# The first chunk of a mixture-of-experts kernel by eight plain products instead of seven Strassen-Winograd ones

## The reference, cut to what matters

```python
def _L0_cond_ref(h, gating_probs, shared_gate_prob, Wg, Wu, Wd, Sg, Su, Sd):
    g = jnp.einsum('bsd,edf->ebsf', h, Wg)          # 8 experts, D=256, F=1024
    u = jnp.einsum('bsd,edf->ebsf', h, Wu)
    expert_outs = jnp.einsum('ebsf,efd->ebsd', jax.nn.silu(g) * u, Wd)
    expert_output = jnp.einsum('be,ebsd->bsd', gating_probs, expert_outs)
    shared = jnp.einsum('bsf,fd->bsd', jax.nn.silu(h @ Sg) * (h @ Su), Sd)
    sg = shared_gate_prob[:, :, None]
    return (1.0 - sg) * expert_output + sg * shared
x = x + _L0_cond_ref(x, fside_Bx8_0, condB_sharedgateprob[:, None], ...)   # x is (16, 256, 256) f32
```

## Time and profile before

| | us |
|---|---|
| median of three runs | 2104.42 |
| the profiled execution | 2105.31 |
| its span, first to last instruction | 2103.5 |
| PE busy in it | 2091.9 (99%) |
| POOL busy | 1611.3 (77%) |
| DVE busy | 1447.7 (69%) |
| ACT busy | 1304.2 (62%) |
| DMA, mean | 206 GB/s |

### The profile page before, as it was taken

One profiled execution on the slowest core, in us unless ns is written; L12 is line 12 of the kernel. 1 busy time (PEld: TensorE's weight loads), 2 busy tenths in 40 slices (PEclk: granted clock), 3 DMA queues, 4 the chain that ended last, 5 costly groups with the idle time before them and its releaser, 6 DMA issues.

```text
span 2103.5 us, 33963 instructions
## 1 busy us (share of the span) xinstructions
PE 2091.9 (99%) x9183; PEld 1719.2 (82%) x9183; DVE 1447.7 (69%) x2630; ACT 1304.2 (62%) x2335; POOL 1611.3 (77%) x1442
## 2 busy tenths in 40 slices
PE   8999999999999999999999999999999999999999
PEld 6888888888888888888888888888888888888887
DVE  7666666666666666666676666666667666666666
ACT  7777777777566555555556655555555555555555
POOL 7988887877488777777778877777777778777776
PEclk9999999999999999999999999999999999999999
DMA  6976666666555455445445446445445445545443
GB/s 221 349 245 238 234 242 230 242 229 232 203 197 209 173 215 209 173 194 209 174 193 210 177 191 229 178 188 209 180 186 210 184 184 210 203 183 209 183 183 143
DMA packets 122747, 433.94 MB, mean 206 GB/s; under 512 B 13760, under 2 KB 41792, under 8 KB 122688
## 3 DMA queue, kind: packets, MB, share of 16 engines
q1 hardware_dynamic: 122688, 433.32, 54.9%
HBM read 329.85 MB, written 103.28 MB: 206 GB/s over the span
## 4 chain that ended last, share of the span: by engine, by line
PE 99%; DVE 1%; issue 0%; ACT 0%; DMA 0%; DVEq 0%; ACTq 0%
PE chain_ps L684 15%; PE chain_ps L685 15%; PE chain_ps L686 15%; PE down_ps L686 8%; PE down_ps L685 8%; PE down_ps L684 8%; PE p_ps L684 6%; PE p_ps L686 6%; PE p_ps L685 6%; PE side_ps L686 4%; PE side_ps L685 4%; PE side_ps L684 4%; DMA acc<-xT 0%; ACT h_forms L1089 0%; DVE acc L1232 0%
## 5 line engine op out<-in xcount | busy, mean ns | idle before, releaser
L455 POOL TENSOR_TENSOR h_forms<-h_t,h_forms 128x512 fp32r<-128x512 f32 x429 | 560.5, 1325 | 269.1 <-ACT h_forms L1089 269.1
L684 PE MATMUL chain_ps<-x_hi,gate_forms 128*128 128x512 f32 x1080 | 422.5, 391 | 0.2
L686 PE MATMUL chain_ps<-x_hi,gate_forms 128*128 128x512 f32 x1080 | 420.7, 390 | 0.0
L685 PE MATMUL chain_ps<-x_lo,gate_forms 128*128 128x512 f32 x1080 | 420.7, 390 | 0.0
L455 POOL TENSOR_TENSOR h_t<-h_b,h_t 128x512 f32<-128x512 f32 x214 | 312.1, 1458 | 73.5 <-DVE h_b L1226 58.2
L1232 DVE TENSOR_TENSOR p_ps<-tap_p,chain_ps 128x512 f32<-128x512 f32 x216 | 150.4, 696 | 247.5 <-PE chain_ps L686 247.5
L1103 ACT COPY chain_ps<-chain_ps 128x512 f32<-128x512 f32 x216 | 123.1, 570 | 281.6 <-DVE h_a L1226 193.9
L1089 ACT CAST h_forms<-h_t 128x512 fp32r<-128x512 f32 x429 | 267.3, 623 | 15.1 <-POOL h_t L455 3.6
L455 POOL TENSOR_TENSOR w_lo<-w_raw,w_hi 128x1152 fp32r<-128x1152 f32 (+2 forms) x74 | 191.9, 2594 | 78.1 <-ACT w_hi L984 77.6
L684 PEld LDWEIGHTS chain_ps<-x_hi,gate_forms 128*128 128x128 f32 x1080 | 202.5, 188 | 54.8 <-ACT chain_ps L1103 5.3
L686 PEld LDWEIGHTS chain_ps<-x_hi,gate_forms 128*128 128x128 f32 x1080 | 202.7, 188 | 43.2
(11 more groups left out here) (117 smaller groups left out, 4878.0 us busy)
## 6 DMA issues: line engine op xcount, KB each, us to landing
gate_forms<-kept_gate SPq DMA_DIRECT2D x216, 896.0 KB, 7.4
down_forms<-kept_down SPq DMA_DIRECT2D x108, 896.0 KB, 4.6
kept_gate<-w_hi SPq DMA_DIRECT2D x72, 448.0 KB, 2.5
kept_gate<-w_lo SPq DMA_DIRECT2D x72, 448.0 KB, 3.1
w_raw<-w SPq DMA_DIRECT2D x72, 256.0 KB, 3.0
w_raw<-w SPq DMA_DIRECT2D x72, 128.0 KB, 2.8
kept_down<-d_hi SPq DMA_DIRECT2D x36, 256.0 KB, 2.3
kept_down<-d_lo SPq DMA_DIRECT2D x36, 256.0 KB, 2.8
```

Of the source, the lines that this page charges most:

```text
L455: return nc.gpsimd.tensor_tensor(dst, a, b, ALU.subtract)
L684: nc.tensor.matmul(bank, w_high, hi, start=start, stop=False, **on)
L685: nc.tensor.matmul(bank, w_high, lo, start=False, stop=False, **on)
L686: return nc.tensor.matmul(bank, w_low, hi, start=False, stop=stop, **on)
```

## The change

Chunk 0 of group 0 is no longer computed by the seven products. PE does eight plain products, `plain_chunk`: 24 matmuls in place of 21. Its first product is written out, and each of its three matmuls waits for its own operand only. The results are gate and up themselves, so that ACT applies the silu straight from the accumulators and the taps, gate sums and up sum of unit 0 go. Chunk 0's S sums are still needed for the stored weights: POOL makes them first thing (`plain_chunk_sums`), and DVE casts and subtracts them late (end of `first_steps`). The lo part of chunk 1's A11, A12 moves from POOL to DVE. B12, until now not needed, gets a hi and a lo part. p4 of unit 0 is gone from between p5 and p6 of unit 1. Chunk 0's stores by SP come behind other loads. All counts of semaphores that unit 0 no longer raises are one lower (`PLAIN`); such lines are left out but for one. Blank lines are left out too.

```diff
-FIRST_X_HI = (B11, T1, B21, B22, T2, T3, T4)
+FIRST_X = (B11, B21, B22, T1, T2, T3, T4)
+PLAIN = 1
...
             def first_keeps():
+                sp.wait_ge(w_lo_done, 1)
+                sp.wait_ge(w1_gate_lo_done, 1)
+                load_blocks(0, 5)
+                sp.wait_ge(w_lo_done, 2)
+                load_blocks(0, 6)
                 sp.wait_ge(w0_lo_done, 4)
                 load_blocks(0, 4)
-                sp.wait_ge(w_lo_done, 1)
-                load_blocks(0, 5)
                 keep_gate(0, 0)
-                keep_down(0, 0)
-                sp.wait_ge(w_lo_done, 2)
-                load_blocks(0, 6)
-                sp.wait_ge(w1_lo_done, 2)
+                sp.wait_ge(w1_lo_done, 1)
                 sp.wait_ge(d_sums, 4)
                 load_down(0, 4)
                 load_down(0, 5)
+                keep_down(0, 0)
...
+            def plain_chunk_sums():
+                def step(dst, a, b, op):
+                    nc.gpsimd.tensor_tensor(raw_of(0, dst, dst), raw_of(0, a, a), raw_of(0, b, b), op).then_inc(w0_sums, 1)
+                pool.wait_ge(w0_lo_done, 2)
+                step(S1, A21, A22, ALU.add)
+                step(S3, A11, A21, ALU.subtract)
+                pool.wait_ge(w0_sums, 1)
+                step(S2, S1, A11, ALU.subtract)
+                pool.wait_ge(w0_sums, 3)
+                step(S4, A12, S2, ALU.subtract)
             def first_chunks():
+                plain_chunk_sums()
                 next_sums(0, 0)
-                pool.wait_ge(w1_hi_done, 1)
-                part_lo(1, A11, A12).then_inc(w1_lo_done, 1)
+                coefficients()
                 pool.wait_ge(w_hi_done, 1)
                 part_lo(1, S3, S4).then_inc(w_lo_done, 1)
-                coefficients()
                 next_sums(0, 1)
                 next_sums(0, 2)
+                pool.wait_ge(w_hi_done, 2)
+                part_lo(2, D0, A22)
                 pool.wait_ge(w_hi_done, 3)
-                part_lo(2, D0, A22)
+                part_lo(2, S1, S4).then_inc(w_lo_done, 1)
                 pool.wait_ge(w_hi_done, 4)
-                part_lo(2, S1, S4).then_inc(w_lo_done, 1)
                 part_lo(1, D0, D1).then_inc(w1_lo_done, 1)
...
             def p4(g, k, n, first=False):
-                pe.wait_ge(up1_done, n + 1)
+                pe.wait_ge(up1_done, n + 1 - PLAIN)
...
             def p1_of(n, k):
                 s = k % SLOTS
-                opening = isinstance(n, int) and n == 0
-                if opening:
-                    first_w(0)
-                elif isinstance(n, int) and n == 1:
-                    pe.wait_ge(w1_lo_done, 1)
+                if isinstance(n, int) and n == 1:
+                    pe.wait_ge(w1_gate_lo_done, 1)
+                    pe.wait_ge(silu_done[0], 1)
                 else:
                     pe.wait_ge(w_lo_done, n)
-                after(pe, h_lo_done[0], n - 1)
-                product(chain_ps[:, k % 2, :], made(s, A11), x_of(0, B11, opening), start=True, stop=True).then_inc(p1_done, 1)
+                    pe.wait_ge(h_lo_done[0], n - 1)
+                product(chain_ps[:, k % 2, :], made(s, A11), x_of(0, B11, False), start=True, stop=True).then_inc(p1_done, 1)
             def p5_of(n, k):
-                opening = isinstance(n, int) and n == 0
-                after(pe, gate1_done, n)
+                opening = isinstance(n, int) and n == 1
                 if opening:
-                    first_w(1)
-                elif isinstance(n, int) and n == 1:
                     pe.wait_ge(w_lo_done, 1)
+                    pe.wait_ge(silu_done[1], 1)
+                else:
+                    pe.wait_ge(gate1_done, n - PLAIN)
                 product(p53_ps[:], made(k % SLOTS, S1), x_of(0, T1, opening), start=True, stop=True).then_inc(p5_done, 1)
...
+            def plain_chunk():
+                gate0, up0, gate1, up1 = chain_ps[:, 1, :], chain_ps[:, 0, :], p53_ps[:], side_ps[:]
+                a11_hi, a11_lo = made(0, A11)
+                pe.wait_ge(x_hi_done, 1)
+                pe.wait_ge(w0_hi_done, 1)
+                nc.tensor.matmul(gate0, a11_hi, x_hi[:, 0, B11, :], start=True, stop=False)
+                b11 = x_of(0, B11, True)
+                nc.tensor.matmul(gate0, a11_hi, b11[1], start=False, stop=False)
+                first_w(0)
+                nc.tensor.matmul(gate0, a11_lo, b11[0], start=False, stop=False)
+                first_w(1)
+                product(up0, made(0, A21), b11, start=True, stop=False)
+                pe.wait_ge(b12_lo_done, 1)
+                b12 = x_hi[:, 1, B11, :], x_lo[:, 1, B11, :]
+                product(gate1, made(0, A11), b12, start=True, stop=False)
+                product(up1, made(0, A21), b12, start=True, stop=False)
+                b22 = x_of(0, B22, True)
+                product(gate1, made(0, A12), b22, start=False, stop=True).then_inc(p3_done, 1)
+                product(up1, made(0, A22), b22, start=False, stop=True).then_inc(p7_done, 1)
+                b21 = x_of(0, B21, True)
+                product(gate0, made(0, A12), b21, start=False, stop=True).then_inc(p2_done, 1)
+                product(up0, made(0, A22), b21, start=False, stop=True).then_inc(p4_done, 1)
             def first_units():
-                p1_of(0, 0)
-                p5_of(0, 0)
-                p2_of(0, 0)
-                p6_of(0, 0)
-                p3_of(0, 0)
-                p7_of(0, 0)
+                plain_chunk()
                 p1_of(1, 1)
                 p5_of(1, 1)
-                p4(0, 0, 0, first=True)
                 p6_of(1, 1)
                 p3_of(1, 1)
                 p2_of(1, 1)
                 p7_of(1, 1)
                 pe.wait_ge(h_lo_done[1], 1)
-                first_w(3)
+                first_w(2)
                 down1(0, start=True, stop=False)
...
-            def first_unit():
+            def first_units():
                 x_form_hi(0, B11)
                 act.wait_ge(w_loaded[0], 16)
                 first_w_hi(A11, A12)
-                act.wait_ge(w0_sums, 4)
-                first_w_hi(S1, S4)
+                first_w_hi(A21, A22)
+                act.wait_ge(x_loaded[1][0], 16)
+                nc.scalar.copy(x_hi[:, 1, B11], acc[:, 1, 0, :]).then_inc(b12_hi_done, 1)
+                x_form_hi(0, B21)
+                x_form_hi(0, B22)
                 x_form_hi(0, T1)
-                x_form_hi(0, B21)
-                tap1(0, 0)
-                x_form_hi(0, B22)
                 act.wait_ge(w_loaded[1], 16)
                 second_w_hi(A11, A12, w1_hi_done)
                 x_form_hi(0, T2)
-                tap5(0)
                 x_form_hi(0, T3)
-                first_w_hi(S3, A22)
+                x_form_hi(0, T4)
+                act.wait_ge(d_loaded[0], 16)
+                first_w_hi(D0, D1)
                 act.wait_ge(w_sums, 4)
                 second_w_hi(S3, S4, w_hi_done)
-                tap_u2_of(0, 0)
-                x_form_hi(0, T4)
+                act.wait_ge(p3_done, 1)
+                nc.scalar.activation(silu[:, 1], p53_ps[:], ACT.Silu).then_inc(silu_done[1], 1)
+                act.wait_ge(p2_done, 1)
+                nc.scalar.activation(silu[:, 0], chain_ps[:, 1, :], ACT.Silu).then_inc(silu_done[0], 1)
+                h1_hi_of(0)
+                tap1(1, 1)
+                tap5(1)
+                weight_hi(0, 2, 0)
+                tap_u2_of(1, 1)
+                weight_hi(0, 2, 1)
+                h0_hi_of(0, 0)
                 act.wait_ge(d_loaded[1], 16)
                 second_w_hi(D0, D1, w_hi_done)
-                act.wait_ge(d_loaded[0], 16)
-                first_w_hi(D0, D1)
-                silu_of(0, 0)
-                silu_of(1, 0)
-            def second_unit():
-                tap1(1, 1)
-                tap5(1)
-                h1_hi_of(0)
-                weight_hi(0, 2, 0)
-                h0_hi_of(0, 0)
-                tap_u2_of(1, 1)
-                weight_hi(0, 2, 1)
                 silu_of(1, 1)
                 silu_of(0, 1)
                 both_hi(HI_BEHIND_UNIT[1])
-            first_unit()
-            second_unit()
+            first_units()
...
                 x_lo_of(B11)
                 w_lo_of(A11, A12, 1)
-                w_sum(S1, A21, A22, ALU.add)
-                w_sum(S3, A11, A21, ALU.subtract)
-                dve.wait_ge(w0_sums, 1)
-                w_sum(S2, S1, A11, ALU.subtract)
-                dve.wait_ge(w0_sums, 3)
-                w_sum(S4, A12, S2, ALU.subtract)
+                w_lo_of(A21, A22, 2)
+                dve.wait_ge(b12_hi_done, 1)
+                minus(x_lo[:, 1, B11], x[0][1], x_hi[:, 1, B11].bitcast(F32)).then_inc(b12_lo_done, 1)
                 dve.wait_ge(x_loaded[0][0], 16)
                 dve.wait_ge(x_loaded[1][0], 16)
                 x_sum_of(0, x[0][1], x[0][0])
-                w_lo_of(S1, S4, 2)
-                x_lo_of(T1)
                 x_lo_of(B21)
+                x_lo_of(B22)
```

(28 more changed lines are left out.)

80 lines of the change are left out of this document (40 added, 40 removed).

## The result

| | before | after |
|---|---|---|
| median of 22 runs, us | 2104.47 (2103.92 to 2105.85) | 2106.90 (2106.01 to 2110.87) |
| the profiled execution, us | 2105.31 | 2106.06 |
| its span, us | 2103.5 | 2104.2 |

The ratio is 1.0014, 95% interval 1.0008 to 1.002: 2.4 us slower, where 1.1 us faster was forecast. That is under 0.2%, yet the two sets of 22 runs do not overlap. The profiled execution is among the three shortest of the changed kernel, and the one of before was among its longer ones: only two of the 22 took more.

A forecast was written before the change was run, and what follows sets the result against it. PE, 99% busy, was taken as the bound; p1 of unit 2 moving from 23.14 to 22.0, with stores costing nothing, gave 1.1 us: 2104.42 - 1.1 = 2103.3 us. Range for all 2101.9 to 2105.0, forecast's own 2102.7 to 2104.0.

The forecast's parts named there:

- 2104.42 - 1.1 = 2103.3 for the median: Final sum: the 1.1 us gained at p1 of unit 2 in the profiled run, taken off the median before.
- p1 of unit 2: First mark on PE: starts at 22.0 us instead of 23.14, held by POOL's lo part; bounds 20.5 to 23.5.
- So the stores just don't cost; the gain stays 1.1: Chunk 0's stores land at 30.1 us, so p6 of unit 3 starts at 32.3, just when PE would come.
- It lands 3.8 us after its issue: Chunk 0's last store, issued by SP at 26.3 us, lands at 30.1, letting ACT cast chunk 4.
- Rival 2: Stores of chunk 0 decide: p6 of unit 3 at 34.2, 0.8 us slower, 2105.2 us; chance 0.15.
- First matmul: PE's start in chunk 0 moves from 5.23 to about 4.8 us, needing only one cast.
- Rise of the clock: PE's clock level rises 6.0 us after unbroken work began, at 10.8 us, or at 14.2 as before.
- ACT's cast of 640 columns: ACT's cast for chunk 1 comes near 13.1 us, behind three token casts, instead of 11.13.
- DVE's last lo part of chunk 0: DVE's late cast and subtraction of chunk 0's S forms end at 23.6 us, before SP's stores.
- Rival 4: First product doesn't start earlier: first matmul at 5.2 us, time still 2103.3; chance within the forecast's 0.45.
- Rival 3: Gain given back to the loads, lo parts late in the second expert: 2104.4 us; chance 0.12.
- PE idles behind 40 us: Sign that the forecast is wrong: PE idle anywhere behind 40 us.

The follow-up runs named there:

- e7: Changed kernel with chunk 0's two down stores issued as soon as DVE has made their lo part; 2106.17 us, ratio 1.0007.
- e12: As e10, with the cast of chunk 0's 640 columns on ACT behind chunk 3's instead of on DVE; 2105.60 us, ratio 0.9999.
- e10: e7 plus ACT's cast of chunk 1's 640 columns moved behind T2 and the two silus of chunk 0 sooner; 2104.38 us, ratio 0.9998.
- e1: The changed kernel once more, unaltered; 2107.67 us, ratio 1.0017.
- e4: Changed kernel with its first matmul also held until B12's lo part is there; 2106.99 us, ratio 1.0014.
- e6: Changed kernel with all semaphore counts as before, nine matmuls of chunk 0 signalling the skipped semaphores; 2107.39 us, ratio 1.0013.
- e3: Changed kernel with chunk 0's down stores directly behind its gate stores, ahead of the down loads of chunks 4 and 5; 2106.73 us, ratio 1.001.
- e8: Changed kernel with the edits of e6 and e7 together: counts as before, chunk 0's down stores early; 2106.60 us, ratio 1.0009.
- e5: The kernel before, unaltered, profiled once more; 2104.91 us, ratio 1.0001.
- e2: The kernel before with only the first product's waits split, each matmul waiting for its own operand; 2104.24 us, ratio 0.9997.

## Why the prediction was wrong

**The step that failed first: "2104.42 - 1.1 = 2103.3 for the median".** The 1.1 us was right against the profiled run, whose mark was at 23.14. But the gain was mostly the removal of that run's accident. Three other executions with before's work there have the mark at 21.64 to 22.00, after has 21.86: against a normal run of before, the plain chunk gains nothing at p1 of unit 2. The row of 2.05 us was read, and used to price collisions; it was not asked whether it is the same in every run, though the run stood 0.9 us above the median, as the prediction itself says.

**The second: "So the stores just don't cost; the gain stays 1.1".** ACT's cast was forecast for 30.1 and came at 30.31, p6 of unit 3 for 32.3 and came at 32.59. That is near, but by luck: the last store was issued at 27.72 and not at 26.3, 3.9 us behind DVE's last lo part instead of 2.7, and it landed 2.5 us later and not 3.8. The two errors cancel. With the landing that the sum took, the cast would have come at 31.5. What failed besides is what follows. "Just don't cost" held for a PE at 33.38 - 1.1 and for that one wait. The lateness went on through POOL (its lo part of chunk 4, its sums of chunk 5) to ACT's cast at 37.94 and PE at 40.73. From p1 of unit 2 to the mark in unit 5 after takes 24.09 us, before 22.70: 1.4 us lost. e7 takes 23.41: it gives back 0.7 by the stores. e12 takes 23.02, 0.4 less than e7 and e10, by POOL.

**The third: a time of landing taken as fixed.** "It lands 3.8 us after its issue" was 2.5 in one run and 4.5 to 4.9 in those near 2110. Rival 2, "the stores decide, and it gets slower", was this mechanism, with a chance of 0.15 and a price of 0.8 us; from p1 of unit 2 to unit 5 it costs 1.4 us in the profiled run and 3.9 to 4.6 in e1, e4 and e6, part of it by the clock, which no term of the sum had. The median of after lies 0.8 us above its profiled run. The mean granted clock of the runs says that most of this, 0.6 us, goes with falls of the clock: the ten runs without one have their median only 0.2 us above the profile. Waits and falls come together, so how much each costs by itself isn't shown run by run; that the stores' place makes the long runs is shown by e3, e7 and e8. 1.4 and 0.8 are 2.2 of the measured 2.4 us.

**What held.** First matmul 4.82 (4.8). Rise of the clock 10.7 (10.8), by luck: in e1, the same program, it came at 9.6 us, and the 6.0 us from which 10.8 was worked out were 3.2 in e5. ACT's cast of 640 columns 12.88 (13.1), p1 of unit 1 14.74 (14.9), p7 18.54 (18.6, though behind idle time, and there was none), p1 of unit 2 21.86 (22.0). DVE's last lo part of chunk 0 ended at 23.86 (23.6). Rival 4 did not occur. Rival 3 did not either: between 60 and 130 us, which holds the second expert, POOL waits 3.9 us for loads (before: 2.9), but PE waits for nothing. Of the forecasts of how it would be proved wrong, one came true: PE idles behind 40 us.

DVE's copy of 640 columns of float32 took 0.98 us beside POOL and 0.69 in e10, the subtraction 0.93 to 0.97. The page "VectorE: DVE Perf Modes" of the Trainium skill (section "Mode 2×_2P") gives such a copy twice the rate; in these rows it has a quarter less time, not half. That doesn't refute the rate: DVE's subtraction takes 0.42 us for 256 columns and 0.68 for 512 (e5), so a part of each duration doesn't shrink with the columns. No row here separates the two.

## What to carry to other kernels

Before a gain is taken off the median, ask how far the profiled run stands from it and which row of it may be an accident; an instruction at four times its usual length is one. An engine that gets ahead of three suppliers wins nothing: mark the same point in each supplier's queue before and after, and look at the one that became later (here POOL, by 1.5 us). A reuse of a buffer that waits for a store needs slack for the slowest landing seen, since in one program it cost 0.2 us in one run (after) and 2.6 in another (e1). And where a forecast hits, check its terms one by one: here two errors of 1.3 us had cancelled.

## What the runs showed of the hardware

- TensorE's clock fell from 2.4 to 1.2 GHz behind idle times of 2.1 and 2.5 us, in e1 and e4, and did not behind one of 2.7 us in e6, nor behind 2.0 us in e7. With a fall, the way from p6 of unit 3 to p6 of unit 4 took 9.2 to 9.3 us, without one 8.1 (e6, after), 7.5 in before. The page "TensorE: Matmul & The Clock Gate" of the Trainium skill (section "What's actually happening") says the chip's observation isn't aligned with the kernel, so that one kernel meets the change at different points in different runs. Before and e5, one program, agree: the level rose at 14.2 and at 11.4 us.
- Which of DVE and POOL comes first, by about 0.1 us, decided 1.6 us of DVE's time: 18.20 against 18.13 gave 2.05 us, and in e2 18.03 against 18.17 gave 0.46. In e5, the same program as before, DVE started 0.70 us ahead and took 0.42.
- The steady loops of one program took 2039.2 us in one execution (before) and 2040.2 in another (e5), as much as the whole change of the opening was thought to be worth.
